# Cross-attention's queries placed straight from their parts into the stacked buffer

## What is computed

```python
qh, kh, vh = (interfere(qh), interfere(kh), interfere(vh))
scores = jnp.einsum('bhqdm,bhkdm->bhqkm', qh, kh) / math.sqrt(dk)
weights = jax.nn.softmax(scores, axis=3)
out = jnp.einsum('bhqkm,bhkdm->bhqdm', weights, vh)
```

## Time and profile before

| | |
|---|---|
| runs, median (lowest to highest) | 3258.55 us (3249.04 to 3259.3) |
| profiled execution, its own time | 3253.99 us |
| its span in the profile | 3252.3 us |
| granted TensorE clock, mean share | 0.994 |
| TensorE matmuls busy | 3192.3 us (98%) |
| VectorE, ScalarE, GpSimd busy | 43%, 37%, 51% |
| moved by DMA | 536.33 MB, 165 GB/s |

### The profile page before, as it was taken

How to read it: one execution, slowest core, us unless ns; L and a number is a source line. 1 busy time by engine, 2 the same in 40 slices (tenths; PEclk the granted TensorE clock), 3 DMA queues, 4 the chain that set the end, 5 groups by cost and what they waited for, 6 DMA issues and landing times. The chain is left out here.

```text
span 3252.3 us, 45378 instructions
## 1 busy us (share of the span) xinstructions
PE 3192.3 (98%) x18212; PEld 2573.9 (79%) x18212; DVE 1411.7 (43%) x2264; ACT 1199.7 (37%) x2427; POOL 1644.6 (51%) x1032
## 2 busy tenths in 40 slices
PE   8999999999999999999999989999999999998999
PEld 6888888888888888888888767777777777776787
DVE  3232242222242223333232336666676766665453
ACT  3223233232332323333333225555565555552100
POOL 4768767687676776865445433333333333231000
PEclk9999999999999999999999989999999999999999
DMA  5333344333435334435444467667768777766142
GB/s 196 103 120 123 121 142 159 123 123 107 136 127 175 123 104 129 137 125 192 143 136 154 148 230 218 221 201 260 230 197 254 231 213 251 237 188 230 62 152 78
DMA packets 176850, 536.33 MB, mean 165 GB/s; under 512 B 21880, under 2 KB 22008, under 8 KB 176648
## 3 DMA queue, kind: packets, MB, share of 16 engines
q1 hardware_dynamic: 174152, 524.86, 49.8%
q10 hardware_dynamic: 2496, 8.65, 0.7%
HBM read 432.51 MB, written 100.14 MB: 164 GB/s over the span
## 5 line engine op out<-in xcount | busy, mean ns | idle before, releaser
L77 PE MATMUL two_ps<-token_halves_h,three_wh 128*128 128x512 f32 x1792 | 713.0, 398 | 8.2 <-DVE token_halves_l L307 3.4
L78 PE MATMUL two_ps<-token_halves_l,three_wh 128*128 128x512 f32 x1792 | 700.1, 391 | 0.0
L79 PE MATMUL two_ps<-token_halves_h,three_wl 128*128 128x512 f32 x1792 | 698.7, 390 | 0.0
L1298 POOL TENSOR_TENSOR ca_probs<-ca_probs,ca_inv 128x512 f32<-128x512 f32 x256 | 267.2, 1053 | 536.0 <-DVE ca_inv L1684 536.0
L569 POOL TENSOR_TENSOR three_wl<-sa_wraw,three_wh 128x1024 fp32r<-128x1024 f32 x192 | 461.9, 2410 | 138.0 <-ACT three_wh L781 138.0
L627 POOL TENSOR_TENSOR halves_l<-sa_praw,halves_h 128x1024 fp32r<-128x1024 f32 x124 | 311.1, 2539 | 393.2 <-ACT halves_h L842 393.2
L953 DVE TENSOR_TENSOR sa_acc<-wide_ps,sa_acc 128x512 f32<-128x512 f32 x256 | 176.8, 691 | 733.0 <-PE wide_ps L79 732.9
L77 PEld LDWEIGHTS two_ps<-token_halves_h,three_wh 128*128 128x128 f32 x1792 | 336.7, 188 | 91.8 <-POOL three_wl L569 9.4
L79 PEld LDWEIGHTS two_ps<-token_halves_h,three_wl 128*128 128x128 f32 x1792 | 336.9, 188 | 72.2
L77 PE MATMUL wide_ps<-halves_h,sa_oh 128*128 128x512 f32 x992 | 390.2, 393 | 2.9 <-DVE sa_acc L953 2.9
L78 PE MATMUL wide_ps<-halves_l,sa_oh 128*128 128x512 f32 x992 | 391.1, 394 | 0.0
(11 more groups left out here) (287 smaller groups left out, 5373.0 us busy)
## 6 DMA issues: line engine op xcount, KB each, us to landing
sa_wraw<-in_wqkv SPq DMA_DIRECT2D x192, 512.0 KB, 3.5
sa_praw<-in_wproj SPq DMA_DIRECT2D x128, 512.0 KB, 3.5
three_wh<-w_folded_hi SPq DMA_DIRECT2D x96, 512.0 KB, 5.8
three_wl<-w_folded_lo SPq DMA_DIRECT2D x96, 512.0 KB, 6.8
ca_kstack<-k_parts SPq DMA_DIRECT2D x192, 128.0 KB, 3.4
ca_qstack<-q_parts SPq DMA_DIRECT2D x93, 256.0 KB, 5.4
ca_owraw<-in_wo SPq DMA_DIRECT2D x32, 512.0 KB, 3.7
tokens<-x SPq DMA_DIRECT2D x28, 512.0 KB, 7.1
```

The source lines that it names most:

```text
L77: nc.tensor.matmul(out, ah, bh, start=(first and i == 0), stop=False)
L78: nc.tensor.matmul(out, ah, bl, start=False, stop=False)
L79: ins = nc.tensor.matmul(out, al, bh, start=False, stop=(last and i == len(parts) - 1))
L1298: nc.gpsimd.tensor_tensor(probs[:, t % 2, js], probs[:, t % 2, js], inv[:, t % 2, js].unsqueeze(2).broadcast_to([P, SH, P]), ALU.mult).the ...
```

## The change

In every step `place_queries` takes the place of the way through memory. SyncE issues the three key loads together, then waits for `qh`, places parts 0 and 1 (eight DMAs), waits for `ql`, and places part 2 (four). The stores, the buffer in memory, `stack_queries` and two semaphores go. TensorE waits for all placements so far, and ScalarE for them ahead of writing `qh`.

```diff
@@ sync
                         sp.wait_ge(k_hi_stored, s.n * 16 + 16)
                         stack_keys(0, k_parts[0])
-                        sp.wait_ge(u_hi, s.n * 2 + 2)
-                        sp.dma_start(q_parts[0], f32(qh[:])).then_inc(q_hi_stored, 16)
                         stack_keys(2, k_parts[0])
-                        sp.wait_ge(u_free, s.n * U + 4)
-                        sp.dma_start(q_parts[1], f32(ql[:])).then_inc(q_lo_stored, 16)
                         sp.wait_ge(k_lo_stored, s.n * 16 + 16)
                         stack_keys(1, k_parts[1])
-                        sp.wait_ge(q_hi_stored, s.n * 16)
-                        stack_queries(0, q_parts[0])
-                        stack_queries(1, q_parts[0])
-                        sp.wait_ge(q_lo_stored, s.n * 16)
-                        stack_queries(2, q_parts[1])
+                        sp.wait_ge(u_hi, s.n * 2 + 2)
+                        place_queries(sp, 0, qh)
+                        place_queries(sp, 1, qh)
+                        sp.wait_ge(u_free, s.n * U + 4)
+                        place_queries(sp, 2, ql)
@@ tensor, scores(0)
-                        pe.wait_ge(q_stacked, QPLACED + m * QSTACK)
+                        pe.wait_ge(q_stacked, n * QPLACED)
@@ scalar, high_unit
                     if s.attn and u == 0:
-                        act.wait_ge(hi_stored, n * 16)
-                        act.wait_ge(lo_stored, n * 16)
-                    elif s.attn and m == 0:
-                        act.wait_ge(q_stacked, QPLACED)
+                        act.wait_ge(k_hi_stored, n * 16)
+                        act.wait_ge(k_lo_stored, n * 16)
                     elif s.attn:
-                        act.wait_ge(hi_stored, m * 16)
-                        act.wait_ge(lo_stored, m * 16)
+                        act.wait_ge(q_stacked, n * QPLACED)
```

More of the change, by code:

```diff
@@ L1015, in __init__, with cross_attention_phase @@
         self.last = self.g == CH - 1 and self.more
-def cross_attention_phase(nc, sems, ident, bias_qkv, eps, x1, ctxT, w_folded_hi, w_folded_lo, wo, k_parts, q_parts,
+def cross_attention_phase(nc, sems, ident, bias_qkv, eps, x1, ctxT, w_folded_hi, w_folded_lo, wo, k_parts,
                           x2, x2_stored, tokens, token_halves, context_halves, wh, wl, uf_hi, uf_lo, vf_hi, vf_lo, ahead_loaded,
@@ L1035, in cross_attention_phase @@
     KSTACK = 16 * PARTS * 2
-    QSTACK = 16 * PARTS
-    QPLACED = QSTACK * PAIRS
+    QPLACED = 16 * PARTS * PAIRS
     STEPS = [CrossStep(n) for n in range(BLOCKS * CH + 1)]
@@ L1100, in cross_attention_phase @@
         k_lo_stored = sem("ca_k_lo_stored")
-        q_hi_stored = sem("ca_q_hi_stored")
-        q_lo_stored = sem("ca_q_lo_stored")
         cleared = sem("ca_cleared")
@@ L1175, in stack_keys @@
                     sp.dma_start(f32(kstack[rows, :, w]), by_slot[w]).then_inc(k_stacked, 16)
-            def stack_queries(a, part):
-                sp.dma_start(f32(qstack[a * PC:(a + 1) * PC]), part.rearrange("(r p) n -> p r n", p=PC)
-                             ).then_inc(q_stacked, 16)
             def store_x2(s, t):
@@ L1519, in step, with high_unit @@
                 n, m = s.n, s.m
-                def high_unit(u, dst, hi_stored, lo_stored):
+                def high_unit(u, dst):
                     if not s.proj:
@@ L1582, in step @@
                     ln.prepare(act, ACT.Exp, 1)
-                    high_unit(0, kh, k_hi_stored, k_lo_stored)
+                    high_unit(0, kh)
                     high_now(*range(ln.GROUPS))
-                    high_unit(1, qh, q_hi_stored, q_lo_stored)
+                    high_unit(1, qh)
                     act.wait_ge(u_hi, 2)
@@ L2098, in decoder_layer @@
     k_parts = nc.dram_tensor("k_parts", (2, P, BT), F32, kind="Internal").ap()
-    q_parts = nc.dram_tensor("q_parts", (2, P, BT), F32, kind="Internal").ap()
     u_hi, u_lo, v_hi, v_lo = [nc.dram_tensor(name, (KC, P, D), F32, kind="Internal").ap()
@@ L2132, in decoder_layer @@
         cross_attention_phase(nc, sems, ident, bias_qkv, eps, x1, a["ctxT"], w_folded_hi, w_folded_lo, a["wo"],
-                              k_parts, q_parts, x2, x2_stored, tokens, token_halves, halves, wh, wl, u_hi, u_lo, v_hi, v_lo, ahead_loaded,
+                              k_parts, x2, x2_stored, tokens, token_halves, halves, wh, wl, u_hi, u_lo, v_hi, v_lo, ahead_loaded,
                               u_loaded, next_w_loaded, two_ps, wide_ps)
```

## The result

The changed kernel took 3273.72 us in the median of five runs (3270.02 to 3278.35), against 3258.55, which is also the median of five (3249.04 to 3259.3): the ratio is 1.0057, 95% interval 1.0046 to 1.0068. It is slower by 0.6%, outside the range that was forecast, on the side that had a chance of 0.12. The profiled execution is the slowest of the five, 3278.35 us, 24.4 us above that of before.

A forecast was written before the change was run, and what follows sets the result against it. TensorE, busy 98% of the span, was taken as the bound, so only its idle time could be won. Terms 2.5 + 0.2 + 0.6 = 3.3 us gave 3255.0 us, range 3247 to 3266.

The forecast's parts named there:

- The placements' price: SyncE's issue in each cross-attention step: 0.62 us per 64 KB placement, so twelve take 7.5 us.
- the short waits before the scores: Scores line, 14 steps: 5.3 us of idle weight loads go as queries land 1.8 us early; worth 2.5 us.
- What SyncE does next is late: Weights and token tile behind the placements: issued later, yet the tile lands 2.9 us into the step; 0.2 us won.
- the issue queue becomes the bound: Rival at SyncE's placements, every step: slower placements make tiles and queries late, some 35 us, 3293 us; chance 0.10.
- The two long waits: Before the scores of steps 10 and 18: waits of 2.98 and 2.56 us stay, only 0.6 us won.
- Moved: costs nothing: Second and third key load pairs, issued ahead of the wait for `qh`: under way during that wait, no cost.
- Engines still full: Rival at the query landing: it stays at 5 us, not 2, as keys, placements and weights share engines; 3258, chance 0.22.
- Block starts recover: Rival at steps 10 and 18: keys and queries arrive 2 us earlier, 5.1 us won there, 3250.8 us; chance 0.12.

The follow-up runs named there:

- The cure by order: Changed kernel with the first two result-tile stores of steps 8, 16 and 24 issued ahead of and between the placements: 3256.35 us, ratio 1.0006.
- the fastest one: Changed kernel with the token tile ahead of the placements and, in steps 8, 16 and 24, two result stores ahead of and between them: 3244.61 us.

## Why the prediction was wrong, point by point

**The placements' price** held, and so did the landing of the last of them. The middle placement took 0.59 us, the mean of 380 was 0.63, and the twelfth landed 2.0 us after issue in most steps. The first ones did not: the first of a step landed a median 4.7 us after issue, the median of all 380 is 3.1 and not the 2 to 2.5 that the prediction named as its sign. Since the scores wait for the last one, this cost nothing. The Trainium skill, "DMA: Bandwidth & Descriptors", section "Bandwidth", gives 0.95 us of moving for 64 KB, from memory to SBUF; it is not the pitch of these placements, which was 0.67 us. (By the prediction's own sum it would have put the queries at 2054.2 + 11.4 = 2065.6, and not at 2066.6.) Of the short waits before the scores, forecast as worth 2.5 us, two came up new (0.5 and 0.6 us ahead of the weight loads), and in all 1.1 us of TensorE's time was won.

**"What SyncE does next is late" is the first step that failed.** It put the tile at 2.9 us into the step, and named a wait for tokens of over 20 us as a sign of being wrong; it was 27.0. In the nine steps it landed 4.1 to 5.8 us in, 5.0 on average. Two sizes were off. The weights were issued 8.2 us behind `qh` on average and not 7.5: in five of the nine steps one placement took 0.4 to 1.0 us longer than the others, and in two SyncE came to the first one 0.7 and 0.9 us after `qh`. And the tile landed 7.8 us after the weights' issue and not 6.2: the 3.7 and 1.25 us came from step 0, where the DMA engines were busy 54% of the time, while between the tile's issue and landing they were busy 98% of it at the turn into step 3:

```profile
1997.88:2004.81 6.93, 6.93 (x36) 5.76 (x35) 3.33 (x5) 3.78 (x11) 1.29 (x1) 1.00 0.98 346
```

The landing is the larger error and would have been enough by itself: 7.5 + 7.8 - 10.9 is 4.4 us into the step, 1.0 past the 3.4 from which a late tile costs. The step had named that point rightly (5.0 less 3.4 us, in nine steps, is 14 us) and left itself 0.5 us of margin, with both of its inputs taken from a quiet stretch of the trace. Its rival, "the issue queue becomes the bound", had the place and the consequence right, but not the threshold: it took over the 6.2 us and so allowed 0.68 us per placement; with 7.8 it would have been 0.54, below the price that the forecast itself used. The placements, 0.67 us with their gap in these nine steps, stayed just under the rival's 0.68, and the tile was late all the same. Term: -0.2 forecast, +13.1 us in the profile (idle ahead of the transposes, 1.9 to 15.0), borne out twice, by 13.2 and 12.1 us, when the tile was issued earlier.

**"The two long waits" is the second step that failed.** It kept the key loads at 2217.01 and worked out only what comes behind them. That part was right: from the first key load to the last landing it gave 12.0 us, and it was 12.4. But SyncE is one queue, and in the step before, the placements push back the store that `load_acc` waits for; all behind it moved 2.7 us. The prediction followed what is queued behind the placements for the weights and the tile, and not for the stores of steps 8, 16 and 24. Term: -0.6 forecast; the waits before the scores of steps 10, 18 and 26 grew by 2.5, 3.1 and 3.5 us, 9 us. The cure by order won 17 us, and going through memory there 13 (10 by the ratios).

**"Moved: costs nothing"** held in the main: the two halves of the edit belong together, and either alone is slower than the kernel before (by 19 us with the keys moved, by 54 with the placements alone). But it rested on SyncE being done with the key loads before `qh`, and in eight of 31 steps, besides the three after a block's end, it came to the placements 0.7 to 1.4 us late.

**"Engines still full"** fell for the queries, which land 2.0 us behind their last issue in most steps; its premise, that keys, placements and weights share the engines, shows in the first placements and in the tile. **"Block starts recover"** went the other way.

**The rest.** From step 1's scores to step 32's the profiled executions differ by 27.1 us. Two windows, with the columns of the earlier trace rows, the kernel before first:

```profile
1935.74:2934.99 999.25, 990.98 (x6668) 779.05 (x6669) 668.39 (x1190) 553.87 (x1513) 361.25 (x302) 0.99 0.73 227
...
1933.87:2960.24 1026.37, 995.58 (x6668) 783.06 (x6669) 668.02 (x1190) 554.63 (x1513) 360.43 (x302) 0.99 0.72 205
```

Of the 27.1 us, 22.5 are idle time of TensorE, nearly all of it the late transposes and the block ends. The other 4.6 us are TensorE busy for longer with the same 6668 matmuls. The granted clock can account for them. Two windows of the changed kernel:

```profile
2501.00:2509.00 8.00, 6.08 (x20) 5.05 (x21) 2.04 (x3) 2.38 (x9) 0.00 (x0) 0.57 0.82 286
2580.00:2584.00 4.00, 4.00 (x23) 2.78 (x25) 1.55 (x3) 2.22 (x6) 2.30 (x2) 0.57 0.38 102
```

The first holds the end of step 18's wait, the second follows 2.25 us of idle TensorE in step 20 (2579.07). In both, the clock is at the lower level, 1.2 GHz, for part of the time. Behind step 1 the kernel before has two such stretches in these steps, of 3.4 us each, near 2231 and 2490; the changed one has four, together 20.5 us. At half speed the 13.7 us more cost at most 6.8 us, less where TensorE stood idle anyway. The version with the result stores between had none from step 2 to step 31, nor had the fastest one, which may be a part of why both won more than expected. That was not tried by itself.

## What to carry to other kernels

Before a queue's work is made longer, list what it issues next and what it *waits* for there, through the next step and at the rare steps too; a blocking wait further on passes the whole delay to everything behind it. A transfer that comes just in time has no margin for a number taken from a quiet stretch: price it where the queue is loaded. And where a change is slower, try the order before giving up the idea: here it was 29 us apart.

## What the runs showed of the hardware

- A DMA from SBUF to SBUF of 32 rows by 2 KB held SyncE for about 0.59 us in 361 of 380 cases, where loads from memory that were issued back to back took about 0.43 each. The Trainium skill, "DMA: Bandwidth & Descriptors", section "Issuing engines are not separate DMA queues", calls the time to initiate a DMA usually small relative to the DMA itself. These are a case where it is not small: 0.59 us of issue where the last four of a burst land 2.0 us after theirs, and twelve hold the issuer for 7.5 us.
- Of 380 placements 19 took 0.8 to 1.8 us. In the packet records 16 of these, all longer than 1.2 us, overlap or directly follow the start of a 16 KB packet of the queue that the page calls instruction (142 of them, 1.1 us each on average). It is a coincidence in time in 16 of 19 cases; no run took those packets away.
- A store from SBUF to memory landed a median 2.1 us after its issue in the kernel before, and 4.9 us in the run with the keys moved alone, where six key loads of 128 KB are issued ahead of it (the store of `qh`, 31 times in each). A wait for it holds everything that SyncE issues next.
- In six of nine steps of the changed kernel the tile landed 2.4 to 3.2 us behind the load ahead of it, where it landed 1.2 to 1.3 us behind it in all nine steps of the kernel before. The DMA engines were busy 98% of that stretch at the turn into step 3. Why it is late is open; the run with the tile ahead of the weights shows only that moving it there is enough.
